# Causal layer: operand loads of later batches issued one group of heads at a time, each after the one in front has landed

## What is computed

```python
logits = jnp.einsum('bhqd,bhkd->bhqk', q, k) * scale          # q, k rotated
probs = jax.nn.softmax(logits + causal_mask, axis=-1)
L = jnp.eye(s) - jnp.tril(probs, -1)
rhs = jnp.diagonal(probs, axis1=-2, axis2=-1)[..., None] * v
A = jax.scipy.linalg.solve_triangular(L, rhs, lower=True)
return A.transpose(0, 2, 1, 3).reshape(b, s, HID) @ Wd.T + bd
```

## Time and profile before

| what | value |
|---|---|
| time, median of 3 runs | 1377.15 us (1373.88 to 1382.85) |
| profiled execution, its own time | 1370.44 us |
| its span (first to last instruction) | 1368.6 us |
| TensorE busy | 1138.3 us (83%) |
| VectorE busy | 979.9 us (72%) |
| ScalarE busy | 686.4 us (50%) |
| GpSimd busy | 619.4 us (45%) |
| DMA queue of SyncE (q1) | 117.65 MB, 30.5% of 16 engines |
| causal layer in the span | about 635 to 1073 us |

### The profile page before, as it was taken

How to read it: one execution, slowest core, us unless ns; L and a number is a source line. 1 busy time by engine, 2 the same in 40 slices (tenths; PEclk the granted TensorE clock), 3 DMA queues, 4 the chain that set the end, 5 groups by cost and what they waited for, 6 DMA issues and landing times. The chain is left out here.

```text
span 1368.6 us, 33177 instructions
## 1 busy us (share of the span) xinstructions
PE 1138.3 (83%) x12993; PEld 616.2 (45%) x13028; DVE 979.9 (72%) x2128; ACT 686.4 (50%) x1425; POOL 619.4 (45%) x828
## 2 busy tenths in 40 slices
PE   6847667768999998797788988988978899999875
PEld 2212232323333333773466666665666333333475
DVE  5699999978888884545775765735725788888453
ACT  3844344424777667441262451442441477666754
POOL 1359999965234321542452362442542233432153
PEclk9969989987999999899989989988989999999988
DMA  5288944231231402227233233141132303140223
GB/s 150 114 296 316 342 185 170 73 80 34 61 94 48 125 9 88 56 66 138 38 71 69 50 64 76 32 95 37 33 84 48 73 2 94 55 122 6 88 63 88
DMA packets 132801, 127.66 MB, mean 93 GB/s; under 512 B 86295, under 2 KB 117847, under 8 KB 128122
## 3 DMA queue, kind: packets, MB, share of 16 engines
q1 hardware_dynamic: 124592, 117.65, 30.5%
q0 software_dynamic: 2496, 5.13, 1.2%
q10 hardware_dynamic: 5558, 2.76, 1.0%
HBM read 104.83 MB, written 37.90 MB: 104 GB/s over the span
## 5 line engine op out<-in xcount | busy, mean ns | idle before, releaser
L1480 DVE TENSOR_REDUCE f_row_min<-f_ps 128x1 f32<-128x512 f32 x480 | 307.2, 680 | 54.1 <-PE f_ps L1811 53.7
L1361 ACT ACTIVATE f_e<-f_ps 128x512 f32<-128x512 f32 x512 | 278.6, 598 | 124.0 <-PE f_ps L1832 123.2
L816 PE MATMUL m_ps<-m_shared,sb_ident 128*128 128x512 f32 x256 | 130.3, 654 | 55.8 <-DVE m_shared L664 53.7
L379 POOL TENSOR_TENSOR m_drive<-m_du,m_ring 128x1024 f32<-128x1024 f32 x64 | 149.7, 2354 | 47.5 <-DVE m_ps L656 31.7
L522 ACT ACTIVATE m_ps<-m_delta,m_A 128x511 f32<-128x511 f32 x128 | 82.9, 681 | 115.6 <-DVE m_ps L656 98.2
L1843 PE MATMUL f_ps<-f_e,f_v_op 128*32 128x512 f32 x1024 | 137.0, 607 | 2.4 <-ACT f_e L1361 1.4
L2707 DVE TENSOR_REDUCE d_row_min<-d_ps 128x1 f32<-128x384 f32 (+3 forms) x176 | 104.5, 630 | 22.5 <-PE d_ps L2945 21.6
L816 PEld LDWEIGHTS m_ps<-m_shared,sb_ident 128*128 128x128 f32 x256 | 50.1, 206 | 138.3 <-DVE m_shared L664 82.6
L656 DVE TENSOR_TENSOR_SCAN m_ps<-m_ps,m_drive 128x1024 f32<-128x1024 f32 x44 | 101.1, 2297 | 5.0
L1811 PE MATMUL f_ps<-f_second_ops 72*128 72x512 bf16 x256 | 98.4, 384 | 2.8 <-DVE f_row_min L1480 2.8
L1811 PE MATMUL f_ps<-first_ops 72*128 72x512 bf16 x224 | 90.4, 412 | 8.9 <-DVE f_row_min L1480 6.5
(11 more groups left out here) (318 smaller groups left out, 2271.4 us busy)
## 6 DMA issues: line engine op xcount, KB each, us to landing
m_ring<-bc_scr SPq DMA_DIRECT2D x32, 1024.0 KB, 5.5
f_rows_scr<-blank SPq DMA_DIRECT2D x2, 8707.5 KB, 32.0
f_wall<-f_wall SPq DMA_DIRECT2D x16, 578.0 KB
first_ops<-q_scr SPq DMA_DIRECT2D x28, 288.0 KB
first_ops<-k_scr SPq DMA_DIRECT2D x84, 96.0 KB
f_second_ops<-q_scr SPq DMA_DIRECT2D x16, 288.0 KB
f_second_ops<-k_scr SPq DMA_DIRECT2D x48, 96.0 KB
f_second_ops<-f_rows_scr SPq DMA_DIRECT2D x36, 64.5 KB, 1.8
```

Source lines behind the costliest of these rows:

```text
L379: nc.gpsimd.tensor_tensor(drive[:, step % AHEAD, :].rearrange("p (a s) -> p a s", a=HALVES), du[:, :, tokens(b)], b_row(step).unsqueeze(1) ...
L816: last = nc.tensor.matmul(bank(Y + k), core.ident[:, :], hC[:, k * S:(k + 1) * S], start=False, stop=last_of_batch)
L1361: nc.scalar.activation(e_sb[:, n % 3, hh, :], ps[:, SCORE[(b * UNITS + u) % SCORE_BANKS], :], ACT.Exp, scale=SCALE).then_inc(s["e_out"], 1)
L1480: nc.vector.tensor_reduce(row_min[:, b % 2, u // TPB, u % TPB:u % TPB + 1], ps[:, MAXQ[unit(b, u) % MAX_BANKS], :], AX.X, ALU.max, negate= ...
```

## The change

`operands(b, g)` gets one more wait. For b of 2 or more, and for every group but the first, SyncE waits until the four DMAs of the group in front, of the same batch, have landed: 16 * (1 + PARTS) * b is 64 b, the value of `op_in{g - 1}` once batch b's loads are in it. Batch 1 is left as it is. Nothing else is changed.

```diff
                 def operands(b, g):
                     sp.wait_ge(s["parts_stored"], 16 * 2 * PARTS * (b + 1))
                     sp.wait_ge(s["act_ps"], in_act("score", b * TPB - 1, DIAG_GROUPS + (g + 1) * GROUP - 1))
+                    if b >= 2 and g >= 1:
+                        sp.wait_ge(s[f"op_in{g - 1}"], 16 * (1 + PARTS) * b)
                     heads = slice(g * GROUP, (g + 1) * GROUP)
                     sp.dma_start(q_op[0:QK_ROWS, heads, :], query_rows(q_scr[b, :, :, heads, :])).then_inc(
                         s[f"op_in{g}"], 16)
```

## The result

The changed kernel takes 1390.43 us (median of 5 runs, 1388.62 to 1392.88) against 1377.44 us for the kernel before (1373.88 to 1382.85): a ratio of 1.0089, 95% interval 1.0057 to 1.0122. In a second comparison on one chip, with 12 runs against 28, it is 1392.63 against 1380.91 us, ratio 1.0074 (1.0043 to 1.0106). It is slower, by about 0.8%. Three later executions lie apart from the rest and are left out of every median and range here: one of the kernel before at 1395 us, one at 2601 us, and one of e10 at 3524 us. The prediction was 1381, range 1371 to 1391: the side was right, the time is inside the range at its upper end, and the loss was three times the 3.9 us of the sum.

A forecast was written before the change was run, and what follows sets the result against it. TensorE was taken as the bound, with the `xT` load behind the operand loads closest to holding it up; 3.9 + 0 + 0 + 1.0 - 1.0 = +3.9 us on the median 1377.15 gave 1381.0 us, range 1371 to 1391.

The forecast's parts named there:

- C: Loading stretches of batch 3 and the last: DMA gaps let TensorE's code through, a gain of 7.5 us, 1369.6; chance 0.12.
- Rival D: Batches 2 and 3: a group's landing takes T = 7.4, `xT` stalls, 19.8 us slower, 1397; chance 0.08.
- signs of being wrong: Line 2942 waits long for group 3, a wait taken for covered shows up, or batch 2's slip is gone by phase's end.
- not additional: Batch 2: group 3 lands 0.9 us after TensorE asks, but TensorE still reaches line 3013 ahead of `xT`.
- T: Distance from one load group to the next with the added wait: 2.1 fixed + 3.4 data = 5.5 us.
- upper bound of 5.9: Largest distance between load groups allowed for: 2.1 fixed + 3.75 us of data, from batch 1's loads.
- Batch 2's queue behind: Batch 2: three waits delay `x_scr` and `xT` behind the loads; TensorE stalls 3.9 us at line 3013.
- Batch 3: Batch 3: the later `xT` stays hidden, 0 us, with 0.8 us to spare.
- Last batch: Last batch: tile 14's later `xT` stays hidden, 0 us, with 1.9 us to spare.
- Code loading: TensorE's "issue" waits while DMA engines are loaded could shrink with loads in single file: -1.0 us.
- The clock: A stall in batch 2 may bring a stretch at half clock: 0 to 2.6 us, taken as 1.0.
- The first step: Line 2942 waits only 0.9 us in all for batches 1 to 3's keys; faster operands have next to nothing to win.

The follow-up runs named there:

- e10: Kernel before with the part stores two steps later and at most two groups of loads in flight: 1376.34 us, ratio 0.9972.
- e7: Changed kernel with half the bytes of the operand loads in batches 2, 3 and the last, same DMAs and waits: 1377.03 us, ratio 0.9955.
- e4: Kernel before with one wait for group 3's landing put behind the loads, ahead of stores, `x_scr` and `xT`: 1383.01 us, ratio 1.0011.
- e3: Kernel before with the added waits in the last batch only: 1377.95 us, ratio 0.9977.
- e12: Kernel before with the added waits in batches 2 and 3, none in the last: 1387.95 us, ratio 1.0077.
- e5: The changed kernel itself, run again beside the kernel before on one chip: 1392.63 us, ratio 1.0074.
- e6: Kernel before with each group from batch 2 on waiting for the group two in front, not one: 1377.12 us, ratio 0.9974.
- e8: Kernel before, no waits, with half the bytes of the operand loads in batches 2, 3 and the last: 1370.23 us, ratio 0.9885.
- e9: Kernel before, no waits, with the six part stores behind the loads put two steps later: 1379.96 us, ratio 0.9999.

## Why the prediction was right in sign and short in size

Slower was right and the time lay in the range, by 0.6 us; the mechanism forecast was not the one that cost the time. That the range held is luck: it was made wide for the comparison's spread and for rivals C and D, and none of these is what happened. Two of the prediction's own signs of being wrong appeared: line 2942 (2944 after) waits long for group 3, and tile 14's `xT` is waited for.

*Where the time is lost: wrong.* The step "not additional" failed. I reckoned that group 3 would land 0.9 us after TensorE asks for it and that `xT` would be the later of the two. It landed 25.3 us after the first issue (816.22 to 841.49), not 22. And TensorE asked sooner than I took from the trace: 21.1 us after the first issue in the kernel before (832.84), but that included 1.9 us of standing for code; in the changed kernel it came to group 2 after 17.0 and to group 3 after 19.3 us. I had the code waits shrinking in one term of the sum and kept them as cover in another.

*The size of T: mis-sized.* The fixed 2.1 us was right (1.9 by e7). The data term was 3.4 and is 4.4 us. Both rows I took it from have groups in flight together. In single file the share of the DMA engines fell to 0.47, so the upper bound of 5.9 was no bound: it should have been left open upwards. With T = 6.3 the prediction's own sum would have been 6.3 + 1.6 + 1.0 - 1.0 = 7.9 us, still all of it at `xT`.

*Batch 2's queue behind: right in mechanism.* The waits moved `x_scr` from 13.0 to 24.8 us after the first load: 11.8, and 3 x (6.3 - 2.3) = 12. It landed in 2.9 us, as taken. The stall on `xT` that follows shows in e4 (2.7 us) and hardly in e7 (0.4); in the changed kernel it is hidden behind the keys.

*Batch 3: wrong.* Predicted 0, found 6.9 us at the keys and 1.1 at `xT`. The argument that its cover is larger held for `xT` only; I did not put the keys' landing there beside TensorE's request.

*Last batch: right in the net, not in its cover.* e3 alone and e12 against e5 show nothing for it. But the 1.9 us to spare were there only because TensorE had stood 2.47 us for code in that one trace: a wait for this `xT` of 0.3 to 4.9 us is in every other trace but e10's, whether its loads wait or not.

*Code loading: right in direction, short in size.* From 800 to 1000 us these waits fell from 11.9 to 5.4 us, 6.5 less, where I had taken 1.0; this offsets part of the 14.6 us of key waits, and may be why they cost only 12 to 13 us. *The clock:* mean granted clock was 0.9038 over the 12 runs of e5 and 0.9093 over 28 of the kernel before. The difference is 2 x 0.0055 of some 1380 us more at half clock, 15 us, of which TensorE would lose half: 8 us at most by this estimate, which takes TensorE for busy all the while. I had 1.0. With the clock at its most the three terms (key waits, code, clock) together exceed the loss, and no run separates them.

*Rival D* (T = 7.4, from 6.4 on over 1%) came near: T is 6.3, and the loss 0.8%. Its place was wrong as the forecast's was. *The first step* of the prediction, that a faster arrival of the operands has next to nothing to win, rested on one trace too: in batch 1, where no wait was added, the kernel before shows 0.3 us of key waits and the other traces 0.6 to 4.7.

## What to carry to other kernels

A wait for landing between transfers that could overlap cost the fixed latency each time here (1.9 us) and the rate too (DMA engines busy 0.42 to 0.47 instead of 0.76): compare the landing of the last one with the moment its reader asks, at each place it is read, before looking at what is queued behind. Work out that moment without the stalls which the same change takes away. If a stream is to be thinned, wait for the transfer two in front: here it kept the engines fed (e6), where one in front lost 0.8%.

## What the runs showed of the hardware that I had not expected

A group of 576 KB alone in flight needs 6.3 us, while four together land in 17.1 us, 4.3 each, or in 19.5 and 17.6 us, where e4 waits for them. Halving the bytes of the operand loads in three batches, with the number of DMAs unchanged, took 10.7 us off a kernel whose TensorE was hardly seen to wait for them in batches 2 and 3. With the bytes, the waits for code during the loads went too, and the mean granted clock was 0.9132 in e8 against 0.9093 over the kernel before. Between 700 and 1060 us the waits for code of 2.4 us and more (up to 3.9) all lie where the DMA engines are busy 0.64 or more, but one of 2.3 us lies where they are busy 0.06 (e9). That loaded engines hold up the code is thus likely, not shown: it rests on few traces, and by which way they would is open.
